# Wider decay rows, nested extra slots, later merging of weights, unread products, and another order in the drain

## What is computed

```python
h = concat([cls_tok, class_token, patches @ W_lin + b_lin]) + position_embeddings   # (64, 38, 256)
# mLSTM: up projection, causal conv of 4 taps + swish, headwise q, k, v, gates
log_f = log_sigmoid(fg); lfm = cumsum(log_f) differences, lower triangle
logD = lfm + ig; mD = max(logD); Dmat = exp(logD - mD)
C = (q @ k.T) * DH ** -0.5 * Dmat
norm = maximum(abs(C.sum(-1)), exp(-mD)); y = C / (norm + 1e-6) @ v
h = h + ((headnorm(y) * norm_w + skip * x_act) * swish(z)) @ W_down
# experts: one shared, one of 32 routed by argmax of x @ gate_w, scaled by its sigmoid
h = h + swiglu(x, shared) + swiglu(x * sigmoid(top logit), expert[top])
```

## Time and profile before

| | us |
|---|---|
| median of 3 runs | 715.77 |
| lowest, highest | 713.05, 715.87 |
| the profiled execution, by the device's time | 711.18 |
| its span, first to last instruction | 709.5 |
| mean granted TensorE clock over the span | 0.953 |

### The profile page before, as it was taken

How to read it: one execution, slowest core, us unless ns; L and a number is a source line. 1 busy time by engine, 2 the same in 40 slices (tenths; PEclk the granted TensorE clock), 3 DMA queues, 4 the chain that set the end, 5 groups by cost and what they waited for, 6 DMA issues and landing times.

```text
span 709.5 us, 11754 instructions
## 1 busy us (share of the span) xinstructions
PE 648.9 (91%) x4013; PEld 548.5 (77%) x4013; DVE 468.7 (66%) x1528; ACT 391.1 (55%) x863; POOL 230.1 (32%) x249
## 2 busy tenths in 40 slices
PE   4899999999999999999999899878899999999892
PEld 3777978868968968968977888856688888888782
DVE  1544767776776777776786875767676776766560
ACT  1337639529529628627637748414566666666560
POOL 4000101143044044044044223253336666332541
PEclk9699599999999999999999989789999999999997
DMA  8239210030030030030010010064799999989950
GB/s 299 90 99 364 68 51 1 14 92 19 7 98 19 1 103 21 1 94 28 2 53 20 2 34 28 19 214 144 258 402 379 380 377 378 351 312 357 324 215 15
DMA packets 46261, 101.69 MB, mean 143 GB/s; under 512 B 10952, under 2 KB 32246, under 8 KB 41329
## 3 DMA queue, kind: packets, MB, share of 16 engines
q1 hardware_dynamic: 35184, 89.07, 34.8%
q0 software_dynamic: 9488, 8.52, 4.5%
q10 hardware_dynamic: 1520, 3.23, 1.3%
HBM read 80.17 MB, written 23.32 MB: 146 GB/s over the span
## 4 chain that ended last, share of the span: by engine, by line
PE 69%; DVE 15%; ACT 6%; issue 3%; DMA 3%; POOL 2%; SPq 0%; DVEq 0%; POOLq 0%
PE bank L1341 14%; PE bank L2190 13%; PE bank L2209 8%; PE bank L1464 5%; PE bank L1309 4%; PE bank L1443 3%; DVE stats_h L946 3%; PE bank L1405 2%; PE bank L1367 2%; PE bank L2198 2%; PE bank L1318 2%; DMA bg<-b_zone_dram 2%; POOL rstd_h L433 2%; PE bank L1436 2%; PE bank L1453 2%
## 5 line engine op out<-in xcount | busy, mean ns | idle before, releaser
L433 POOL TENSOR_TENSOR rstd_h<-var_h,minus_half 76x4 f32<-76x4 f32 x32 | 32.3, 1009 | 193.0 <-DVE var_h L960 193.0
L2009 POOL DMA_INDIRECT out<-rows,bg x32 | 37.7, 1179 | 69.5 <-DVE rows L2080 62.6
L2190 PE MATMUL bank<-w_hi,x_hi 128*128 128x512 f32 x148 | 56.6, 463 | 3.2 <-DVE x_lo L2092 2.9
L1309 PE MATMUL bank<-patch,lin_w 128*128 128x288 f32 x192 | 51.6, 423 | 8.2 <-DMA col_t<-cols 7.8
L1309 PEld LDWEIGHTS bank<-patch,lin_w 128*128 128x128 f32 x192 | 36.8, 198 | 19.8 <-POOL v L410 7.8
L864 DVE SCALAR_TENSOR_TENSOR y<-xm,conv_t,y 128x296 f32<-128x296 f32 (+2 forms) x96 | 43.7, 511 | 9.1 <-ACT xm L483 9.1
L1796 POOL DMA_INDIRECT x_zone_dram<-xs_rows,spot x32 | 39.6, 1238 | 26.8 <-DVE spot L1054 9.2
L2190 PE MATMUL bank<-w_lo,x_hi 128*128 128x512 f32 x148 | 46.3, 394 | 0.0
L483 ACT ACTIVATE att_t<-bank 128x304 f32<-128x304 f32 x15 | 6.3, 423 | 72.3 <-PE bank L1464 71.7
L2190 PE MATMUL bank<-w_hi,x_lo 128*128 128x512 f32 x148 | 46.2, 393 | 0.0
L1796 POOL DMA_INDIRECT b_zone_dram<-base_rows,spot x32 | 37.2, 1162 | 25.8 <-DVE base_rows L1075 17.3
(11 more groups left out here) (250 smaller groups left out, 1792.7 us busy)
## 6 DMA issues: line engine op xcount, KB each, us to landing
wts<-w_exp SPq DMA_DIRECT2D x18, 1024.0 KB, 10.6
x_act<-w_exp SPq DMA_DIRECT2D x10, 1024.0 KB, 9.2
silu_z<-w_exp SPq DMA_DIRECT2D x9, 1024.0 KB, 9.7
wts_down<-w_exp SPq DMA_DIRECT2D x18, 512.0 KB, 8.4
patch<-patches SPq DMA_DIRECT2D x8, 864.0 KB, 6.5
down_w<-w_exp SPq DMA_DIRECT2D x10, 512.0 KB, 9.0
lin_w<-w_exp SPq DMA_DIRECT2D x9, 512.0 KB, 9.6
b_zone_dram<-act_t SPq DMA_DIRECT2D x1, 4160.0 KB, 28.2
```

The lines of the kernel that those rows point to most:

```text
L433: pool.tensor_tensor(rstd_h[:, j, :], var_h[:, j, :], minus_half[:], ALU.pow).then_inc(s_rstdh, 1)
L1309: last = pe.matmul(fb[c][:, 0:GS * N], lin_w[:, k, c * 128:(c + 1) * 128], patch[:, k, :], start=(k == 0), stop=(k == KF - 1))
L2009: pool.indirect_dma_start(out, bass.IndirectOffsetOnAxis(ap=rows_at, axis=0), rows[:, k % 4, :], None, bounds_check=T - 1, oob_is_err=Fals ...
L2190: last = pe.matmul(banks[2 + 2 * e + u][:, :], x[:, e, c * SLOT:(c + 1) * SLOT], w[:, e, u, c * I:(c + 1) * I], start=(n == 0), stop=(n == ...
```

## The change

Seven edits. (1) `AT` grows from 48 to 76: `pick`, `top_parts`, the gates' transpose and the transpose back are 76 rows or columns; the added ones hold zeros. (2) `merge_weights` of the first front moves on TensorE from behind the transposes of `xn` to behind `up(f, 3)`, on DVE behind the first six convolution steps but two; its raw weights lie in `q_t`. (3) In the step with f = 1 the convolution steps of lags 2 and 3 and the two `x_act_of` move to the end of the step, and in the step with a = 0 `heads` 2 and 3 stand ahead of `up(f, 5)`. (4) `stream` issues products of the identity with 512 columns of weights that nobody reads: four ahead of the first transposes of `xn`, one ahead of `mixed_gate_weights`, one behind the decay tiles of the second drain, two around the last group's transposes. (5) In the drain `ranks` moves behind `up(f, 6)`; `route` moves between decay tiles 1 and 2 and writes another bank; `gate_up(m, 0)` stands between the heads; on DVE `norm_1` goes ahead of `base_of`, the low parts ahead of `top_gates`, and the last convolution ahead of `expert_act(m, 3)`. (6) The checks of the extra slots are nested, so that the first unused one leaves all. (7) SP issues the weights of the first extra slots among the loads of the last four experts.

```diff
-AT = LOW + NT * NH
+AT = R
-        q_raw = within(y, "p k s t -> p (k s t)", 0, [KI, 128])
-        k_raw = within(y, "p k s t -> p (k s t)", KI * 128, [KI, 128])
+        q_raw = within(q_t, "p h j t -> p (h j t)", 0, [KI, 128])
+        k_raw = within(q_t, "p h j t -> p (h j t)", KI * 128, [KI, 128])
@@ ScalarE step
-                if f: x_act_of(f, 0)
+                if f and f.n != 1: x_act_of(f, 0)
...
+                if f and f.n == 1:
+                    x_act_of(f, 0)
+                    x_act_of(f, 1)
                 if m: ffn_t_of(m)
@@ VectorE step
-                if f and f.n == 0: merge_weights()
                 if m: xn2_lo_of(m)
...
-                if f:
+                if f and f.n != 1:
                     conv_of(f, 0, (2, 3))
                     conv_of(f, 1, (1,))
+                if f and f.n == 0: merge_weights()
                 if m: expert_act(m, 1)
-                if f: conv_of(f, 1, (2, 3))
+                if f and f.n != 1: conv_of(f, 1, (2, 3))
...
                     last_channel(a, 3)
+                if f and f.n == 1:
+                    conv_of(f, 0, (2, 3))
+                    conv_of(f, 1, (1,))
                 if m: base_of(m)
                 if a: state(a)
+                if f and f.n == 1: conv_of(f, 1, (2, 3))
@@ VectorE drain
             conv_of(f, 1, (1,))
+            conv_of(f, 1, (2, 3))
             expert_act(m, 3)
-            conv_of(f, 1, (2, 3))
...
+            xn2_lo_of(m)
             top_gates(a)
-            xn2_lo_of(m)
+            norm_1(a)
             base_of(near)
-            norm_1(a)
             weigh(a, 0)
             route(m)
@@ TensorE
+            def stream(bank, moving, times):
+                for _ in range(times):
+                    pe.matmul(bank[:, :], ident[:], moving[:, 0:2, :].rearrange("p k d -> p (k d)"),
+                              start=True, stop=True)
-                pe.transpose(ab[3][0:R, 0:NT * NH], top_gate[0:NT * NH, :],
-                             ident[0:NT * NH, 0:NT * NH]).then_inc(s_top_mm, 1)
+                pe.transpose(ab[3][0:R, 0:AT], top_gate[:], ident[0:AT, 0:AT]).then_inc(s_top_mm, 1)
@@ TensorE step
+                if f and f.n == 0: stream(ab[3], lin_w, 4)
                 if f: to_columns(fb, xn, s_xn, f.n, s_xnt_mm)
-                if f and f.n == 0: merge_weights()
...
                 if f: up(f, 3)
+                if f and f.n == 0: merge_weights()
...
+                if a and a.n == 0:
+                    heads(a, 2)
+                    heads(a, 3)
                 if f: up(f, 5)
-                if a:
+                if a and a.n > 0:
...
                     turn_up()
+                    stream(ab[3], lin_w, 1)
                     mixed_gate_weights()
@@ TensorE drain
-            ranks(m)
             mixed_gates(f)
             up(f, 6)
+            ranks(m)
...
             decay(a, 1)
+            route(m)
             decay(a, 2)
             decay(a, 3)
-            route(m)
+            stream(fb[1], sd_w, 1)
             heads(a, 0)
             heads(a, 1)
+            gate_up(m, 0)
             heads(a, 2)
             heads(a, 3)
-            gate_up(m, 0)
...
             m = last
+            stream(ab[1], sd_w, 1)
             to_columns(fb, xn2, s_xn2, m.n, s_xn2t_mm)
+            stream(ab[1], sd_w, 1)
             route(m)
@@ extra slots, TensorE, VectorE and ScalarE (GpSimd alike)
-            for k in range(E, ALL):
-                with eng.If(extra > k - E):
+            with ExitStack() as deep:
+                for k in range(E, ALL):
+                    deep.enter_context(eng.If(extra > k - E))
                     turn(k, extra)
@@ SyncE loads
-            for k in range(E - 2):
-                if k + 4 < E: load_x(k + 4)
+            for k in range(E - 4):
+                load_x(k + 4)
...
-            load_base(E - 1)
             extra = extra_slots(sp)
-            for k in range(E, ALL):
+            def load_late_gate_up(k):
                 with sp.If(extra > k - E):
                     load_gate_up(k, sort.load_late, k - E)
-                    load_down(k, sort.load_late, k - E)
+                sp.nop()
+            for k in range(E - 4, E):
+                if k + 2 < E:
+                    load_down(k + 2, sort.load, k + 2)
+                else:
+                    with sp.If(extra > k + 2 - E):
+                        load_down(k + 2, sort.load_late, k + 2 - E)
+                    sp.nop()
+                load_late_gate_up(k + 4)
+                if k + 1 < E: load_base(k + 1)
+            with ExitStack() as deep:
+                for k in range(E, ALL - 2):
+                    deep.enter_context(sp.If(extra > k + 2 - E))
+                    load_down(k + 2, sort.load_late, k + 2 - E)
+                    if k + 4 < ALL: load_late_gate_up(k + 4)
```

More of the change, by code:

```diff
@@ L654, in step @@
                 if m: silu_g_of(m, 3)
-                if f: x_act_of(f, 1)
+                if f and f.n != 1: x_act_of(f, 1)
                 if m: score_rows(m)
@@ L908, in top_gates @@
                 dve.wait_ge(s_parts, 2 * a.n + 1)
-                dve.tensor_tensor(top_parts[LOW:, :], top_gate[LOW:, :], top_parts[LOW:, :].bitcast(f32),
+                low = slice(LOW, LOW + NT * NH)
+                dve.tensor_tensor(top_parts[low, :], top_gate[low, :], top_parts[low, :].bitcast(f32),
                                   ALU.subtract).then_inc(s_parts, 1)
@@ L1021, in route @@
                 dve.wait_ge(s_rt_mm, m.n + 1)
-                parts = mb[0][0:R, 0:2 * NT * E].rearrange("p (j u e) -> p j e u", j=NT, u=2)
+                parts = xn2_banks(m)[0][0:R, 0:2 * NT * E].rearrange("p (j u e) -> p j e u", j=NT, u=2)
                 dve.tensor_reduce(logits[:], parts, AX.X, ALU.add).then_inc(s_lgt, 1)
@@ L1480, in route @@
                     for c in range(KD):
-                        pe.matmul(mb[0][0:R, 2 * j * E:2 * (j + 1) * E], xn2_hi[:, c, tile], route_w[:, c],
+                        pe.matmul(xn2_banks(m)[0][0:R, 2 * j * E:2 * (j + 1) * E], xn2_hi[:, c, tile], route_w[:, c],
                                   start=(c == 0), stop=False)
                     for c in range(KD):
-                        last = pe.matmul(mb[0][0:R, 2 * j * E:(2 * j + 1) * E], xn2_lo[:, c, tile],
+                        last = pe.matmul(xn2_banks(m)[0][0:R, 2 * j * E:(2 * j + 1) * E], xn2_lo[:, c, tile],
                                          route_w[:, c, 0:E], start=False, stop=(c == KD - 1))
@@ L1985, in _ @@
             load_base(0)
-            for k in range(E - 2):
-                if k + 4 < E: load_x(k + 4)
+            for k in range(E - 4):
+                load_x(k + 4)
                 load_down(k + 2, sort.load, k + 2)
-                if k + 4 < E: load_gate_up(k + 4, sort.load, k + 4)
+                load_gate_up(k + 4, sort.load, k + 4)
                 load_base(k + 1)
-            load_base(E - 1)
             extra = extra_slots(sp)
-            for k in range(E, ALL):
+            def load_late_gate_up(k):
                 with sp.If(extra > k - E):
                     load_gate_up(k, sort.load_late, k - E)
-                    load_down(k, sort.load_late, k - E)
+                sp.nop()
[13 more added lines that the diff above has]
+                    if k + 4 < ALL: load_late_gate_up(k + 4)
         @block.gpsimd
@@ L2061, in _ @@
                 scatter(k, bg[:, k % 4, D:D + 1].bitcast(u32))
-            for k in range(E, ALL):
-                with pool.If(extra > k - E):
+            with ExitStack() as deep:
+                for k in range(E, ALL):
+                    deep.enter_context(pool.If(extra > k - E))
                     gather_ahead(k, extra)
```

## The result

The changed kernel took 687.83 us in the median of 4 runs (685.75 to 692.2), beside 714.96 for the kernel before. The ratio, with its interval of 95%, is 0.9656 [0.9613, 0.9699], which is 24.6 us; the two medians differ by 27.1. The forecast was 702.6, with a range down to 695.5. The profiled executions took 711.18 and 689.14, spans 709.5 and 687.4, so 22.0 of the 27.1 us are seen in them.

What follows compares the result with a forecast made beforehand. TensorE was taken to bound the kernel, with 58 us of stretches at half clock. The terms summed to 13.2 us, subtracted from the median of 715.8 for 702.6 us; the range was 695.5 to 709.5.

Steps and rivals of the forecast that it cites:

- Wider rows: All 8 groups: wider transpose back and weight load cost 0.3 us; what they bring to the clock counted in other terms.
- What moves nothing there moves little: From 89.24 to 406.69 us, at 2.4 GHz with TensorE busy 300.62 of 317.45: edits not moving this stretch gain little.
- Second step: Step with 17.06 us at half clock: reordering frees VectorE but TensorE was just as late; gain 0, bounds -1.7 and 3.9.
- Drain: Two drain steps, groups 7 and 6: reordering fills waits, gains 1.1 and 2.0 us; bounds for both together 0 and 5.
- Tail: Unused slots at the end: one exit replaces 13 branches, GpSimd is late next; gain 2.5 us, bounds 0.4 to 3.7.
- Late loads: Extra-slot turns: earlier weight loads remove ScalarE's waits, turns return to 5.26 us; gain 2.7 us, bounds 1.0 and 2.7.
- End of the first step: Ahead of `mixed_gate_weights`: one stream keeps the clock, half of 3.41 us won; 1.5 net, otherwise 0.2 lost.
- Last group: Around its transposes: two streams hidden in waits avert the 6.82 us half stretch; gain 2.1 us, bounds -0.3 and 3.0.
- First step: Before group 1's embedding: streams fit the wait, `up(f, 0)` starts ahead of the merging; gain 1.6 us, bounds -3.4 to 3.4.
- The clock is held in the second step and the drain too, 696.5: Rival: no half clock in the second step and second drain, 3.9 + 1 + 1.2 us more; chance 0.15.
- The slots don't do what they say: Rival: long jump paid in full, loads only move the stall to GpSimd's gathered rows; 707.4 us, chance 0.1.
- The slower rival: Middle groups lose the clock, 3.4 us per fall; six groups give 723.0 us, chance 0.04.

Runs made afterwards that it cites:

- wide_only: Kernel before with only the decay rows widened from 48 to 76 and the transpose back at 76 columns: ratio 0.9929 [0.9893, 0.9965].
- loads_only: Kernel before with only the earlier weight loads of the extra slots: one execution, 705.14 us beside a median of 711.04.
- second trace: Changed kernel, nothing altered, profiled and compared once more: ratio to the kernel before 0.9643 [0.9595, 0.9690], span 686.9 us.
- nested_only: Kernel before with only the nested checks of the extra slots, on every engine: one execution, 705.51 us beside a median of 711.04.
- drain_only: Kernel before with only the new order of the two drain steps and the new bank of `route`: ratio 0.9975 [0.9942, 1.0008].
- fill_all: Changed kernel with unread products in three more waits (five, three and two): ratio to the kernel before 0.9647 [0.9616, 0.9678].

## Why the prediction was wrong in its size

- **Wider rows (-0.3): the step that failed.** It priced what the edit adds, columns of a transpose and of a weight load, and took it for granted that a `pick` product of 48 rows costs what its own length says. (Its 0.05 us for the transposes is that of one group; eight are 0.4, which changes little.) The trace of before would have shown otherwise: the first `pick` starts 0.25 us behind a mask of 304 columns, where products with as many columns in the up projection start 0.14 apart (340.53 and 340.81 for a pair and the next). In its place: 1.1 us a group on TensorE, 0.75 of it on the path; 5 us by the medians alone, 10 together with the rest.
- **"What moves nothing there moves little"** was the sentence that hid it: between 90 and 400 us the forecast looked only at the clock, not for a change in each of the groups.
- **Second step (0; bounds -1.7 and 3.9).** Right in one trace (17.07 us at half, -0.5), at its upper bound in the other (6.83 at half, 3.9). No cause in the edit is shown; the wait that precedes the fall is.
- **Drain (1.1 and 2.0).** The waits went as said, and the norm was late next with 1.08. But the sum kept the first half stretch of 6.82 and half the price of the second, of 10.24; one trace has them at 6.83 and 3.41, the other not at all. Measured 1.9 and 2.9 in the one, 4.2 and 3.9 in the other. The upper bound of 5 for both holds for the first, with 4.8, and not for the second, with 8.1: it left out that the first stretch too can be absent, and the wider rows, with which this step is 40.8 us long in wide_only, without a half stretch, against 44.9 before.
- **Tail (2.5; bounds 0.4 and 3.7).** Mechanism right, size off: GpSimd's jump costs next to nothing, and its drain starts 5.6 us behind the last product where it started 8.0. Of these 2.5 us the checks are 1.9, near the 12 × 0.15 = 1.8 of the forecast; another 0.6 lies ahead of the first check. Measured 4.2, above the bound of 3.7; the 2.5 was a choice between two outcomes, and the better one came.
- **Late loads (2.7)** 2.7 in loads_only. **End of the first step (1.5)** 1.7, with the half stretch near 51.7 gone. **Last group (2.1)** 2.2. All three as reckoned.
- **First step (1.6)** 1.1, and 2.0 in the second trace: size right, reason half wrong. The falls at 24.89 and 35.13 are where they were forecast; the second trace has one, at 25.92. But with the streams in place moving the merging gave nothing.
- **Rivals.** "The clock is held in the second step and the drain too, 696.5" was the nearest, and its mechanism shows in single executions. "The slots don't do what they say" fell. The slower rival's mechanism, a fall in a middle group, came once (106.81, 1.8 us) in the profiled execution; nested_only and drain_only, with narrow rows, have one there too (112.76, 110.83), so it doesn't take the wide rows. With this one and the shorter stretch of the second step, two of the forecast's signs of being wrong were there; neither points at the rows.
- **The base.** Subtracting a saving of the profiled execution from the median was right by chance at best: the terms of single executions move by 4 us with where the clock falls.

By the ratios the parts alone sum to 5.1 (rows) + 5.6 (unread products) + 1.8 (drain) and, by the traces, 4.2 + 2.7 (slots), 19.4 in all, under the 24.6 and 25.5 that the ratios give for all together; undone one by one, the rows, the unread products and the drain's order cost 10.3, 5.1 and 6.6 by the ratios. What is left, 5 to 6 us, is no more than the intervals of the parts allow, 2 to 3 us each way for every one. It may be nothing, or the parts acting together through the clock; no run shows which.

## What to carry to other kernels

Where short products of different heights alternate, read the starts of consecutive groups and compare with what the instructions take; here padding 48 rows to 66, 76 or 128 with zeros bought 0.27 us for each tile. Price an edit that is made in every group in the groups that nobody complains of, before the rare places. A half stretch of the clock is worth only what no other wait takes back: look, as in fill_all, at what is late next, and don't take one trace's stretches for the kernel's.

## What the runs showed of the hardware

- Products of 48 or 64 rows beside one of 76: the tile of one mask and four picks takes 0.64 us with 48 or 64 rows, 0.37 to 0.38 with 66, 76 or 128. A difference between 76 and 128 costs nothing. With 48 rows the first `pick` weight load starts with its own product, with 76 with the mask's.
- TensorE's far branch costs 3.4 to 3.8 us once, GpSimd's, ScalarE's and VectorE's 0.05 to 0.06.
- The same program has its half clock stretches at other places from one execution to the next, 27.3 and 23.9 us in the two traces of the changed kernel, with nearly the same span.
